# Attention without loops, with the scores of four heads made together and the masked scores kept in SBUF

## What is computed

```python
B, L, D = x.shape                # 4, 2048, 256;  H = 16 heads, dh = 64
bl = 128; nb = L // bl; G = L // 16
q = einsum('bld,dhk->blhk', x, Wq) / sqrt(dh)    # k, v the same way
g = einsum('bgd', sums of x over 16 tokens)      # side tokens, 128 of them
side_k, side_v = g @ Wk, g @ Wv
# queries of one block of 128 see the block before, their own, the next one,
# masked to a distance of at most 127, and all 128 side tokens
logits = einsum('bnqhd,bnkhd->bnhqk', qb, k_cat) + bias
m = max(logits.max(-1), 0)
probs = exp(logits - m) / (exp(logits - m).sum(-1) + exp(-m))
y = einsum('bnhqk,bnkhd->bnqhd', probs, v_cat)
return einsum('blhk,hkd->bld', y, Wo)
```

## Time and profile before

| | |
|---|---|
| median of 3 runs | 2498.21 us (2495.73 to 2502.98) |
| the profiled execution, its own time | 2508.59 us |
| its span, first to last instruction | 2506.5 us |
| attention in it | about 445 to 2205 us of the span |
| granted TensorE clock, mean | 0.978 |

### The profile page before, as it was taken

The page is one execution under the profiler, slowest core; times in us unless marked ns, Lnnn a source line. Parts: engine busy times, 40 slices in busy tenths (PEclk is TensorE's granted clock), DMA queues, the critical chain, the costliest instruction groups (busy, mean ns, idle before and its releaser), DMA issues. The chain is left out here.

```text
span 2506.5 us, 98603 instructions
## 1 busy us (share of the span) xinstructions
PE 2198.1 (88%) x34394; PEld 1693.7 (68%) x34394; DVE 1893.7 (76%) x4448; ACT 2140.6 (85%) x4422; POOL 1638.5 (65%) x1453
## 2 busy tenths in 40 slices
PE   1888885899899889999988998998899999979998
PEld 0555553677777767777776777777677777746666
DVE  6789986687687767777776876877677777758876
ACT  2988882899899879989987998998799899869998
POOL 1677775577677657767765776776576677647765
PEclk9999996999999999999999999999999999989999
DMA  5100000999999999999999999999999999911001
GB/s 186 49 0 0 0 1 18 144 160 159 146 162 162 160 141 160 160 148 163 163 159 140 161 162 149 162 158 156 144 162 156 158 158 160 157 32 34 33 25 42
DMA packets 1111389, 300.24 MB, mean 120 GB/s; under 512 B 1091440, under 2 KB 1109872, under 8 KB 1110896
## 3 DMA queue, kind: packets, MB, share of 16 engines
q1 hardware_dynamic: 1110896, 294.00, 77.9%
HBM read 14.68 MB, written 8.39 MB: 9 GB/s over the span
## 5 line engine op out<-in xcount | busy, mean ns | idle before, releaser
L987 POOL TENSOR_TENSOR probs_split<-probs,probs_split 128x512 f16<-128x512 f32 (+1 forms) x1026 | 1156.6, 1127 | 578.8 <-ACT probs_split L1267 577.2
L1313 DVE CUSTOM_DVE_ANT_0 score_ps<-score_ps,mask,neg_qk_scale 128x512 f32<-128x512 f32 (+1 forms) x1028 | 750.0, 730 | 337.1 <-PE score_ps L1091 319.8
L1267 ACT ACTIVATE probs_split<-probs 128x512 f16<-128x512 f32 (+1 forms) x1026 | 632.3, 616 | 133.9 <-ACT probs L1252 93.8
L1252 ACT ACTIVATE probs<-score_ps,minus_max 128x512 f32<-128x512 f32 (+1 forms) x1027 | 683.4, 665 | 54.9 <-DVE minus_max L1313 49.4
L1109 PE MATMUL y_ps<-v_parts,probsT 128*128 128x64 f16 x11922 | 520.1, 194 | 96.7 <-DMA probsT<-probs_split 93.3
L1109 PEld LDWEIGHTS y_ps<-v_parts,probsT 128*128 128x128 f16 x11922 | 455.8, 98 | 215.1 <-DMA probsT<-probs_split 157.2
L1088 PE MATMUL score_ps<-k_parts,q_parts 64*128 64x128 f16 (+1 forms) x4524 | 420.7, 235 | 30.7 <-issue 25.1
L1091 PE MATMUL score_ps<-k_parts,q_parts 64*128 64x128 f16 (+1 forms) x4524 | 420.7, 235 | 0.0
L1088 PEld LDWEIGHTS score_ps<-k_parts,q_parts 64*128 64x128 f16 x4524 | 279.2, 94 | 73.9 <-issue 35.8
L1091 PEld LDWEIGHTS score_ps<-k_parts,q_parts 64*128 64x128 f16 x4524 | 279.2, 94 | 0.0
L1020 PE MATMUL item_ps<-b_xT,wk_split 128*128 128x128 f16 x3168 | 223.0, 221 | 13.3 <-DVE b_xT L1305 6.5
(11 more groups left out here) (173 smaller groups left out, 3969.2 us busy)
## 6 DMA issues: line engine op xcount, KB each, us to landing
probsT<-probs_split SPq DMA_TRANSPOSE x1033, 4.1
out_x<-x_resident SPq DMA_DIRECT2D x16, 512.0 KB, 2.9
x_resident<-in_L_attn_x SPq DMA_DIRECT2D x14, 512.0 KB, 4.3
raw_up<-in_L_ffn_w_up SPq DMA_DIRECT2D x1, 1024.0 KB, 5.7
raw_down<-in_L_ffn_w_down SPq DMA_DIRECT2D x1, 1024.0 KB, 7.6
raw_q<-in_L_attn_Wq SPq DMA_DIRECT2D x1, 1024.0 KB, 9.5
raw_k<-in_L_attn_Wk SPq DMA_DIRECT2D x1, 1024.0 KB, 11.5
raw_v<-in_L_attn_Wv SPq DMA_DIRECT2D x1, 1024.0 KB, 13.2
```

Of the source, the lines that this page charges most:

```text
L987: nc.gpsimd.tensor_tensor(parts_of[v % NPARTS][:, LO, cols], probs[v % NBUF][:, cols], parts_of[v % NPARTS][:, HI, cols], ALU.subtract).th ...
L1252: nc.scalar.activation(probs[v % NBUF][:, cols], score_ps[v % NBUF][:, cols], ACT.Exp, bias=bias[:, j % 2, h:h + 1], scale=-1.0, accum_out ...
L1267: nc.scalar.activation(parts_of[v % NPARTS][:, HI, cols], probs[v % NBUF][:, cols], ACT.Copy).then_inc(phi_done.sem, 1)
L1313: nc.vector.tensor_tensor_reduce(out=score_ps[v % NBUF][:, cols], in0=score_ps[v % NBUF][:, cols], in1=w.mask[:, cols], scale=w.neg_qk_sca ...
```

## The change

Four edits in `attention_phase`, and nothing outside it. The loops over batches and rounds are unrolled by Python, so that all values of waits are constants. The `separate` increments are gone. DVE writes the masked scores into the SBUF tile `probs[v % 4]` in place of their PSUM bank, ACT's exp reads and writes that tile, the wait on `plo_done` moves from ACT to DVE, and PE's wait for a free bank goes from `exp_done` to `max_done`. PE makes the scores of four heads, in two pairs, at every fourth unit in place of two at every second.

```diff
-            with eng.Fori(0, BATCH) as b:
-                body(At(b, 0), b)
-                with eng.Fori(1, ROUNDS - 1) as i:
+            for b in range(BATCH):
+                for i in range(ROUNDS):
                     body(At(b, i), b)
-                body(At(b, ROUNDS - 1), b)
...
                 plo_done.wait(sp, at.heads + v)
-                separate(sp)
                 pv_done.wait(sp, at.heads + v - NBUF)
-                separate(sp)
                 sp.dma_start_transpose(pt[v % NBUF][:], parts_of[v % NPARTS][:].rearrange("p s n -> p (s n)")
...
                 if v >= NBUF:
-                    exp_done.wait(pe, at.heads + v + 1 - NBUF)
+                    max_done.wait(pe, at.heads + v + 1 - NBUF)
...
-                    if u % 2 == 0:
-                        scores(at, u + SCORE_AHEAD)
+                    if u % NBUF == 0:
+                        for pair in range(0, NBUF, 2):
+                            scores(at, u + SCORE_AHEAD + pair)
...
                 cols = columns(place_of(at, v))
-                separate(act)
-                plo_done.wait(act, at.heads + v - NBUF)
-                separate(act)
-                nc.scalar.activation(probs[v % NBUF][:, cols], score_ps[v % NBUF][:, cols], ACT.Exp, bias=bias[:, j % 2, h:h + 1],
+                nc.scalar.activation(probs[v % NBUF][:, cols], probs[v % NBUF][:, cols], ACT.Exp, bias=bias[:, j % 2, h:h + 1],
...
                 exp_done.wait(act, at.heads + v)
-                separate(act)
                 act.wait_ge(turned[v % NPARTS], turn_count(at, v - NPARTS))
-                separate(act)
...
                 scores_done.wait(dve, at.heads + v)
-                separate(dve)
-                nc.vector.tensor_tensor_reduce(out=score_ps[v % NBUF][:, cols], in0=score_ps[v % NBUF][:, cols],
+                plo_done.wait(dve, at.heads + v - NBUF)
+                nc.vector.tensor_tensor_reduce(out=probs[v % NBUF][:, cols], in0=score_ps[v % NBUF][:, cols],
```

More of the change, by code:

```diff
@@ L811, in attention_phase @@
         y_cleared = sem("y_cleared")
-        passed = sem("b_passed")
         block = ctx.enter_context(nc.Block())
-        def separate(eng):
-            eng.sem_inc(passed, 1)
         class At:
```

## The result

| | before | after |
|---|---|---|
| median | 2497.86 us | 2380.8 us (2378.53 to 2383.6) |
| ratio | | 0.9529, 95% interval 0.9511 to 0.9547 |
| profiled execution, span | 2506.5 us | 2381.9 us |
| instructions executed | 98603 | 86866 |

The change takes 117 us off. Forecast were 83, in a range of 23 to 148; the narrower range that the prediction calls its own, 2394 to 2441 us, was missed by 13 us. The difference lies in the attention: in the profiles the first transpose starts at 451 and 455 us, and from the last one to the end it takes 303 us in both.

A forecast was written before the change was run, and what follows sets the result against it. SP's transpose issue was taken as the bound at 1.649 us a head, ACT right behind. 43 us for the jumps plus 40 for a pace of 1.61 made 83, median 2415 us; own range 2394 to 2441, wider range 2350 to 2475.

The forecast's parts named there:

- The seams: Jumps back between attention rounds: unrolling removes the cost of seven, 43 us, bounds 37 and 43.
- SP's stream: Steps between transpose issues on SP: 0.12 to 0.13 us a head goes of 0.25, bounds 0 and 0.25.
- SP is full; the transposes set the pace: Attention between jumps: SP issues one transpose each 1.676 us without real gaps, so it bounds the kernel.
- SP still without waits while issues stretch: Sign on SP's queue that the forecast is wrong and only the jumps' cost goes.
- Exp from SBUF: ACT's exp reading SBUF instead of PSUM: 679 to about 723 ns, +0.044 us a head, bounds 0 and 0.044.
- ACT's self-wait: split_high waiting behind exp on ACT: 0.20 to 0.08 us, saving 0.053 us a head, between 0 and 0.09.
- ACT's floor: ACT's busy time plus its own waits: 1.60 us a head before, 1.59 after, bounds 1.51 and 1.645.
- The coupling: Engines waiting for each other: 0.05 us a head above ACT's floor, of which 0.02 stays after the change.
- The sum: Whole attention: 1.649 to 1.61 us a head gives 40 us, with the jumps 83 us, median 2415.
- Only the seams go: Rival: the pace between jumps stays at 1.649 us a head, 2455 or 2461 us; chance 0.27.
- More goes: Rival: exp from SBUF costs nothing, ACT's waits shrink, PE and SP hold 1.55 us a head, 2354 us; chance 0.13.
- Slower: the group head stands: Rival: PE stands at every fourth unit for a late mask, 97 us in half of 256 groups, 2552 us; chance 0.12.

The follow-up runs named there:

- unroll_spfree: The kernel before with loops unrolled by Python and the two separate increments removed from SP alone, kept on ACT and DVE: 2422.01 us, ratio 0.9671.
- unroll_nosep: The kernel before, unrolled and without separate increments in the attention, but with the old data flow and scores in pairs: 2383.05 us, ratio 0.9534.
- pairs_sbuf: The changed kernel with scores made in pairs at every second unit again, masked scores still in SBUF: 2383.06 us, ratio 0.9534.
- four_psum: The changed kernel with masked scores back in their PSUM bank, freed by exp, and groups of four kept: 2410.05 us, ratio 0.9648.
- after_trim: The changed kernel with transposes of 768 in place of 1024 columns for the 128 heads whose fourth tile is empty: 2373.67 us, ratio 0.949.
- half_after: The changed kernel with each transpose cut to the high parts, half the size, low parts stale, so results are wrong: 2351.84 us, ratio 0.9401.
- after_sepsp: The changed kernel with the two separate increments put back on SP alone: 2410.31 us, ratio 0.9624.

## Why the prediction was right, and where it was off

- **The seams, 43 us.** Held: with the count mended they are 47, and from 470 us to the attention's end no engine stands longer than 3 us. One stand of 4.32 us is left on ACT, up to 459.9 us near the attention's start. The lower bound of 37 took the earlier trace rows for all seven: ACT's stands are 3.1 to 5.5 us, 32.5 in all. And the prediction left out the clock. In the kernel before, TensorE's granted clock fell to its lower level (1.2 of 2.4 GHz) for 3 to 7 us at six of the seven jumps, after PE had stood for 3.1 to 4.7 us; from 470 us to the attention's end the changed kernel has the full clock throughout. Before, at the jump of the earlier trace rows (engines, clock and DMA as in the earlier trace rows):

```profile
1326.00:1328.00 2.00, 0.41 (x8) 0.42 (x10) 0.00 (x0) 0.00 (x0) 0.00 (x0) 0.70 0.36 82
1328.00:1330.00 2.00, 2.00 (x21) 1.53 (x18) 0.29 (x1) 0.17 (x1) 0.00 (x0) 0.50 0.06 12
```

  How much of the 47 us is clock and how much standing, no run tells apart.
- **SP's stream, 0.12 to 0.13 us of 0.25.** The steps gave 0.16, and the mean issue took 0.04 of it back. The step that failed is the one before it: "SP is full; the transposes set the pace". Full it was, but a queue can be full and hold little of the pace. unroll_spfree gives 17 us for its two increments, and putting them back costs 24, in part because the issues change their length against the steps. One sign was ill chosen: "SP still without waits while issues stretch" came true, and the pace fell all the same.
- **Exp from SBUF, +0.044 us.** The row has 710 - 679 = 0.031. The accumulator's read went from 197 to 189 ns and the split from 630 to 625, so ACT's busy time a head rose by 0.01 only (1.53 to 1.54, below). The side of it that mattered I had missed: the time comes back as less waiting for DVE (unroll_nosep against the changed kernel), so it costs nothing.
- **ACT's self-wait, 0.20 to 0.08 us, 0.053 a head.** It is 0.03, so 0.17 x 53/120 = 0.075. Here the sum was too small. ACT's floor, by my own rule of busy time and its own waits, I had at 1.59. Measured over nearly the whole attention it is 1555.06/1009 = 1.54:

```profile
469.00:2069.00 1600.00, 1521.95 (x29852) 1278.66 (x29847) 1299.76 (x3293) 1555.06 (x3733) 1174.29 (x1072) 1.00 1.14 168
```

  The same rule over the eight stretches of the earlier trace rows gives 994.5/649 = 1.53 of busy time and 0.09 of self-wait, 1.62 and not the 1.60 that I started from.
- **The coupling.** I had kept 0.02 us of waiting above ACT's floor; it is 1.586 - 1.54 = 0.04, as much as before (1.66 - 1.62). "With the tighter coupling gone" was wrong: pairs_sbuf and unroll_nosep show that groups of four and the freer bank loosened nothing that held. DVE's waits for PE did shrink, as forecast (16.9 us for the 37.1 in the earlier trace rows), but nobody had been waiting for that. DVE's new wait for POOL cost nothing, as forecast: the stretch shows none.
- **The sum.** 1.61 us a head forecast, 1.586 measured; 1.649 taken for before, 1.66 in truth. (1.66 - 1.586) x 1024 = 76 and 47 make 123 in the profiled executions, whose spans differ by 125; the medians differ by 117. The forecast's 40 for the pace was half of what came, and the mis-sized terms are ACT's self-wait (22 us too little), the exp (0.044 where ACT's busy time rose by 0.01, some 35 us too much) and the floor that stood on both. The coupling, 0.02 us too small, hid 20 us of that: that the sum is not farther off is in part luck, since these errors offset each other.
- **The rivals.** *Only the seams go* is out. *More goes*, 2354, is as near to the 2381 as the forecast of 2415: ACT's waits shrank as it says. *Slower: the group head stands* needs the bank to be freed by exp: four_psum shows it, at 29 us and not at 97. The Trainium skill, "Advanced Engine Details and Errata", section TRN2 Errata, says that ScalarE is closer to PSUM and VectorE closer to SBUF; the exp row agrees, 31 ns, and so does DVE's mask, 10 ns shorter when it writes SBUF. It decided nothing.

## What to carry to other kernels

Small queue instructions around a wait cost time where the wait is short and often: on ACT, which was 96% spoken for, two increments around a wait for the engine's own last result cost 53 us, and having exp read its tile from SBUF and not from PSUM cost nothing that could be measured. Before a busy queue is taken for the bound, put a known delay on it and look at how much of it comes through; here it was 70% on ACT and a quarter on SP, though SP looked the fuller. And where engines run a fixed number of units apart, an order that spares one engine a wait can be slower, here by 72 us; that it was slower because each unit's way round became longer is argued, not shown.

## What the runs showed of the hardware

- The issue of a DMA transpose on SP took 1.29 us in the median for 1024 columns (changed kernel), 1.24 for 768 (after_trim) and 1.22 for 512 (half_after). The size shows little on the issuing queue; it shows on the DMA engines (a share of 1.12 for 1024 and 0.54 for 512 columns) and in the landing (4.1 and 2.5 us).
- The length of an issue isn't fixed: for the same 1024 columns its mean was 1.400 us with 0.25 us between issues (before), 1.438 with 0.09 (changed kernel) and 1.407 with 0.18 (after_sepsp).
- An ACT instruction that carries the wait for the result just ahead of it starts 0.03 us after that; with two semaphore increments between, 0.20 us.
- exp of 128x512 took 679 ns from PSUM and 710 from SBUF. DVE's mask, mean 730 ns with all forms when it wrote PSUM, took 720 when it wrote SBUF, and the read of its accumulator behind it 82 ns in the median where it had been 141.

DVE's row of the profile after:

```profile
L1300 DVE CUSTOM_DVE_ANT_0 probs<-score_ps,mask,neg_qk_scale 128x512 f32<-128x512 f32 (+1 forms) x1028 | 740.0, 720 | 140.7 <-PE score_ps L1082 138.3
```

- Seven jumps back stood for some 47 us, 6 to 7 us each; ACT's own stand is 3.1 to 5.5 us, 32.5 in all, and at six of them the granted clock fell to its lower level for 3 to 7 us.
